# Tiles of 125 partitions moved in two transfers of 112 and 13 partitions, in a two-layer graph network on one core

## The reference, cut to what matters

```
xn = layernorm(x)
x = x + graph0(xn, edges) + linear_attention(xn)
x = x + experts0(layernorm(x))
xn = layernorm(x)
x = x + graph1(xn, edges) + flow_attention(xn)      # graph1: two attention layers over the edges,
x = x + experts1(layernorm(x))                      # the first with 4 heads of 512 features, the second with one of 768
```

## Time and profile before

| | |
|---|---|
| median of 3 runs | 3583.74 us (3577.38 to 3588.89) |
| the profiled execution's own time | 3586.41 us |
| its span | 3584.6 us |
| PE busy | 2857.5 us (80%) |
| DVE busy | 1539.8 us (43%) |
| ACT busy | 809.5 us (23%) |
| mean granted TensorE clock | 0.877 of full speed |
| moved by DMA | 314.12 MB, mean 88 GB/s |

### The profile page before, as it was taken

How to read it: one execution, slowest core, us unless ns; L and a number is a source line. 1 busy time by engine, 2 the same in 40 slices (tenths; PEclk the granted TensorE clock), 3 DMA queues, 4 the chain that set the end, 5 groups by cost and what they waited for, 6 DMA issues and landing times. The chain is left out here.

```text
span 3584.6 us, 32335 instructions
## 1 busy us (share of the span) xinstructions
PE 2857.5 (80%) x12086; PEld 2117.3 (59%) x12086; DVE 1539.8 (43%) x2325; ACT 809.5 (23%) x1117; POOL 259.9 (7%) x251
## 2 busy tenths in 40 slices
PE   4998687989449956999899769995972976928884
PEld 2564355578449934966587535553972536727773
DVE  2214886332425434123227068883126533215554
ACT  1000012020125502211222234442102111014451
POOL 0000000000110020000000033330002200020002
PEclk9999898999569957988799989996985986969996
DMA  4400002120078631100113121103211001066664
GB/s 158 166 14 14 3 17 81 68 96 1 17 255 285 224 96 67 32 18 12 61 62 122 65 85 61 61 30 106 67 54 48 0 1 53 1 182 223 234 214 152
DMA packets 110467, 314.12 MB, mean 88 GB/s; under 512 B 40860, under 2 KB 50741, under 8 KB 101156
## 3 DMA queue, kind: packets, MB, share of 16 engines
q1 hardware_dynamic: 70572, 224.26, 18.1%
q10 hardware_dynamic: 21856, 57.43, 4.3%
q0 software_dynamic: 17920, 30.81, 3.2%
HBM read 215.33 MB, written 97.05 MB: 87 GB/s over the span
## 5 line engine op out<-in xcount | busy, mean ns | idle before, releaser
L2021 PE MATMUL ps<-g_p,g_h 125*128 125x418 f32 x960 | 341.8, 516 | 50.3 <-DMA g_h<-h_projected 50.3
L2021 PEld LDWEIGHTS ps<-g_p,g_h 125*128 125x128 f32 x960 | 182.8, 191 | 207.1 <-issue 156.3
L1043 PE MATMUL ps<-e_wh,e_xh 128*128 128x384 f32 (+1 forms) x600 | 221.0, 368 | 0.5 <-DVE e_wl L1262 0.5
L1043 PE MATMUL ps<-e_wh,e_xl 128*128 128x384 f32 (+1 forms) x600 | 214.7, 358 | 0.0
L1043 PE MATMUL ps<-e_wl,e_xh 128*128 128x384 f32 (+1 forms) x600 | 214.3, 357 | 0.0
L215 PE MATMUL ps<-la_w,normed 128*125 128x384 f32 x480 | 156.6, 490 | 6.7 <-DMA la_w<-in_L_kv 6.7
L1272 DVE TENSOR_TENSOR e_xl<-ps,e_xh 128x768 fp32r<-128x768 f32 x68 | 65.1, 958 | 214.6 <-ACT e_xh L1213 214.6
L1140 PE MATMUL ps<-ident,e_x 128*128 128x128 f32 x408 | 59.1, 284 | 114.1 <-DMA e_x<-expert_rows 114.1
L1043 PE MATMUL ps<-w_hi,h_hi 128*125 128x384 f32 x320 | 114.0, 356 | 42.1 <-DVE w_lo L2609 42.0
L2297 PE MATMUL ps<-g_p,normed 125*128 125x418 f32 x360 | 130.1, 523 | 19.5 <-DVE g_p L2476 19.5
L2112 DVE SCALAR_TENSOR_TENSOR ps<-g_rows,g_logits,normed 125x418 f32<-125x418 f32 x120 | 127.1, 1068 | 33.0 <-DMA g_bias<-in_L_b 15.6
(11 more groups left out here) (413 smaller groups left out, 5825.1 us busy)
## 6 DMA issues: line engine op xcount, KB each, us to landing
e_w<-in_L_experts SPq DMA_DIRECT2D x32, 1152.0 KB, 6.2
e_w<-in_L_experts SPq DMA_DIRECT2D x18, 1536.0 KB, 7.1
e_x<-expert_rows SPq DMA_DIRECT2D x68, 384.0 KB, 5.2
expert_rows<-e_y ACTq DMA_DIRECT2D x68, 384.0 KB, 3.7
expert_rows<-attT ACTq DMA_DIRECT2D x13, 1536.0 KB, 6.6
e_w<-in_L_experts SPq DMA_DIRECT2D x18, 768.0 KB, 5.2
h<-normed SPq DMA_DIRECT2D x48, 209.0 KB, 1.9
h_projected<-gp_h ACTq DMA_DIRECT2D x40, 250.0 KB
```

The source lines that it names most:

```text
L1043: mm = nc.tensor.matmul(out, lhs[a], rhs[b], start=(start and m == 0), stop=(stop and m == 2))
L2021: mm = nc.tensor.matmul(ps[:, f, 0:CW], h_sb[:, i % 2, t, P * f:P * f + P], pr[:, n % 2, t, :], start=(t == 0), stop=(t == TILES - 1))
```

## The change

A helper `two_parts` issues two transfers where there was one: partitions 0 to 111, then partitions 112 to 124, on the same queue, to the same semaphore. Every wait on such a semaphore asks for 32 where it asked for 16. No buffer, order or arithmetic changes. Loads of 125 partitions that are left as they were: the edges, the attention vectors (`a_rows`) and a small bias. There are 41 such transfers on SP (x 2, masks out 10, counts out 1, masks in 10 and 10, counts in 3 and 1, features 4) and 40 on ACT (the feature tiles), so 81 issues more.

```diff
+def two_parts(eng, dst, src, sem):
+
+    for part in (slice(0, 112), slice(112, NT)):
+        eng.dma_start(dst[part], src[part]).then_inc(sem, 16)
...
-                    sp.dma_start(k.x_node[:, 5 * g:5 * g + 5, :],
-                                 x_dram[625 * g:625 * g + 625, :].rearrange("(t p) d -> p t d", p=NT)).then_inc(loaded[g], 16)
+                    two_parts(sp, k.x_node[:, 5 * g:5 * g + 5, :],
+                              x_dram[625 * g:625 * g + 625, :].rearrange("(t p) d -> p t d", p=NT), loaded[g])
...
-                    dve.wait_ge(loaded[t // 5], 16)
+                    dve.wait_ge(loaded[t // 5], 32)
...
-                    sp.dma_start(k.far_dram[t], far[:, t % 2, 0:T]).then_inc(far_out[t % 2], 16)
+                    two_parts(sp, k.far_dram[t], far[:, t % 2, 0:T], far_out[t % 2])
                 for h in range(2):
-                    sp.wait_ge(far_out[h], 16 * (TILES // 2))
+                    sp.wait_ge(far_out[h], 32 * (TILES // 2))
...
-                sp.dma_start(k.counts_dram[:, :, :], whole[:]).then_inc(kept, 16)
+                two_parts(sp, k.counts_dram, whole[:], kept)
...
-                        sp.dma_start(far[:, t % 2, :], k.far_dram[t]).then_inc(far_in[t % 2], 16)
+                        two_parts(sp, far[:, t % 2, :], k.far_dram[t], far_in[t % 2])
...
-                        act.wait_ge(st[n % HR], 16 * (n // HR))
+                        act.wait_ge(st[n % HR], 32 * (n // HR))
...
-                    act.dma_start(h_dram[n // TILES, :, n % TILES, :], h[:, n % HR, :]).then_inc(st[n % HR], 16)
+                    two_parts(act, h_dram[n // TILES, :, n % TILES, :], h[:, n % HR, :], st[n % HR])
...
-                    sp.dma_start(h_sb[:, i % 2], h_dram[i]).then_inc(h_in[i % 2], 16)
+                    two_parts(sp, h_sb[:, i % 2], h_dram[i], h_in[i % 2])
...
-                    sp.dma_start(counts[:, a:b, :], k.counts_dram[:, a:b, :]).then_inc(c_in[q], 16)
+                    two_parts(sp, counts[:, a:b, :], k.counts_dram[:, a:b, :], c_in[q])
...
-                        sp.dma_start(far[:, n % 2, :], k.far_dram[t]).then_inc(far_in[n % 2], 16)
+                        two_parts(sp, far[:, n % 2, :], k.far_dram[t], far_in[n % 2])
...
-                sp.dma_start(counts[:], k.counts_dram[:, :, :]).then_inc(c_in, 16)
+                two_parts(sp, counts[:], k.counts_dram, c_in)
```

More of the change, by code:

```diff
@@ L447, in rows_out @@
                     if t >= 2:
-                        dve.wait_ge(far_out[t % 2], 16 * (t // 2))
+                        dve.wait_ge(far_out[t % 2], 32 * (t // 2))
                     nc.vector.tensor_reduce(k.dinv[:, t:t + 1], st[:, t % 2, 0:T], AX_X, ALU.add).then_inc(summed, 1)
@@ L562, in _ @@
                 sp.wait_ge(cast, TILES)
-                sp.dma_start(k.counts_dram[:, :, :], whole[:]).then_inc(kept, 16)
+                two_parts(sp, k.counts_dram, whole[:], kept)
                 for i in range(1, heads):
                     weights_in(i)
-                sp.wait_ge(kept, 16)
+                sp.wait_ge(kept, 32)
             @block.vector
@@ L1890, in _ @@
                     if n >= HR:
-                        act.wait_ge(st[n % HR], 16 * (n // HR))
+                        act.wait_ge(st[n % HR], 32 * (n // HR))
                     nc.scalar.activation(h[:, n % HR, :], ps[0:NT, n % 4, 0:F], ACT.Copy).then_inc(out, 1)
                     act.wait_ge(out, n + 1)
-                    act.dma_start(h_dram[n // TILES, :, n % TILES, :], h[:, n % HR, :]).then_inc(st[n % HR], 16)
+                    two_parts(act, h_dram[n // TILES, :, n % TILES, :], h[:, n % HR, :], st[n % HR])
                     extra(n)
                 for q in range(HR):
-                    act.wait_ge(st[q], 16 * len(range(q, N, HR)))
+                    act.wait_ge(st[q], 32 * len(range(q, N, HR)))
             @block.vector
@@ L1924, in _ @@
                 for t in range(TILES):
-                    dve.wait_ge(far_in[t % 2], 16 * (t // 2 + 1))
+                    dve.wait_ge(far_in[t % 2], 32 * (t // 2 + 1))
                     for i in range(heads):
@@ L2015, in _ @@
                             if n % CH == 0:
-                                pe.wait_ge(h_in[i % 2], 16 * (i // 2 + 1))
+                                pe.wait_ge(h_in[i % 2], 32 * (i // 2 + 1))
                             pe.wait_ge(s["p_made"], TILES * (n + 1))
@@ L2118, in weights @@
                                 if m == a:
-                                    dve.wait_ge(c_in[q], 16)
+                                    dve.wait_ge(c_in[q], 32)
                             nc.vector.scalar_tensor_tensor(out=pr[:, n % 2, t - 2, :], in0=t1(m), scalar=1.0,
@@ L2433, in maxima @@
                         n = i * TILES + t
-                        dve.wait_ge(far_in[n % 2], 16 * (n // 2 + 1))
+                        dve.wait_ge(far_in[n % 2], 32 * (n // 2 + 1))
                         nc.vector.tensor_tensor_reduce(mscr, rows[0:NT, i % 2, 0, 0:T], far[:, n % 2, :], 1.0, 3 * BIG, ALU.add, ALU.max,
@@ L2520, in _ @@
                 dve.wait_ge(b_in, 16)
-                dve.wait_ge(c_in, 16)
+                dve.wait_ge(c_in, 32)
                 weights(0, 0)
```

## The result

| | before | after |
|---|---|---|
| median of 4 runs of each | 3582.34 us (3577.38 to 3588.89) | 3540.61 us (3534.80 to 3548.74) |
| ratio | | 0.9888, 95% interval 0.9868 to 0.9909 |
| span of the profiled execution | 3584.6 us | 3537.6 us |
| PE busy | 2857.5 us | 2853.5 us |

The kernel is 41.7 us faster by the medians. The forecast was 3530 us with a range of 3516 to 3548: the time lies inside it, but of the 54 us in the sum some 42 came (33 to 47 by the interval of the ratio). The profile after says where the missing 12 are.

What follows compares the result with a forecast made beforehand. Waits for 125-partition transfers, on five of sixteen engines, were taken as what the change could shorten, with PE busy 80%. 20 + 25 + 6.5 + 2.5 = 54 us off 3586.41 gave 3532.4, forecast as 3530 us, range 3516 to 3548.

Steps and rivals of the forecast that it cites:

- No change: Rival: parts of 112 stay on five engines and the issues are hidden; time within 0.3% of the old; chance 0.05.
- a middle spread of eight engines: Rival: the fullest engine has 14 + 2 partitions; about 28 us gained, 3556 us; chance 0.06.
- serial parts: Rival: parts move at the old pace, the second after the first; 20 us added, 3604 us; chance 0.04.
- the share: Sign of being right: DMA share near 0.9 to 1.0 during the load of x, at about 400 GB/s.
- the statistics near 9 us: Sign of being right: DVE's statistics of x begin near 9 us and end near 18 to 21 us.
- DVE's weights as PE's releaser: Sign of being right, first four-head graph layer: weights release PE instead of features; its 50.3 us idle shrinks to about 25.
- the features still release PE: Sign of being wrong, first four-head graph layer: PE still waits for the features, near 2070 us or later.
- 8 x 15,360 bytes at 25.8 GB/s: Step for each half of x: the fullest engine has 8 partitions, so the flow takes 4.8 us instead of 15.2.
- x: Term for the load of x at the start: halves land at 8.9 and 13.7 us, statistics end earlier; 20 us.
- The first four-head layer: Term for counts and features in the first graph layer of four heads: PE starts earlier, at 2066.2; 25 us.
- The masks of the last layer: Term for DVE's two mask buffers: two masks take 5.1 us instead of 6.34; 6.5 us.
- Ends of two stages: Term: last mask wait in the counts stage about 1.3, last ACT store in the projection stage about 1.2; together 2.5 us.

Runs made afterwards that it cites:

- The cut at 115: The same two transfers as in the change, cut at 115 partitions instead of 112; ratio 1.0018 to the kernel before.
- The places run: Six loads of 983,040 bytes without the network, on 16, 32 and 64 partitions, neighbours or spread; 109 against 198, 200 against 384, 204 against 415 GB/s.
- The padded kernel: The kernel before with every transfer that the change cuts as one of 128 partitions, three of them padding; 3531.07 us, ratio 0.9861.

## Why the prediction was right, and what it mis-sized

**The reason held.** Five engines carried a tile of 125 partitions, the parts of 112 use all sixteen (share near 1), and what waited for such a tile gained. The cut at 115 shows that it is the divisor that counts, not that there are two transfers. No change, a middle spread of eight engines and serial parts are out.

Of the signs named beforehand the share, the masks and the projection stage came out, the last with no idle time left in PE's costliest group there:

```profile
L1049 PE MATMUL ps<-gp_w_hi,normed_hi 128*125 128x512 f32 x240 | 96.2, 401 | 0.0
```

The 400 GB/s, the statistics near 9 us and DVE's weights as PE's releaser did not. One sign of being wrong came true: the features still release PE, 26.9 us after the first issue, which on the clock of the kernel before is 2073.

**The step that was mis-sized** is the pace: "8 x 15,360 bytes at 25.8 GB/s". The 25.8 came from loads of 128 partitions. With 112 partitions sixteen engines work, but they move 290 GB/s in the stretch of x shown above instead of 412, and 247 over the load of the four-head layer. The places run shows that the pace depends on which partitions are written. That with 112 several engines meet at one place of the on-chip memory and wait for each other fits this, but it is inferred: that run had no load of 112. The bounds were taken from one kind of row, and both ends (25.8 and 20.7 GB/s for each engine) came from transfers of 128 partitions, so they did not bound this case. Term by term:

- *x*: forecast 20 us, bounds 18.4 to 20.8; measured 13.6, and 12.9 for the whole when done alone.
- *The first four-head layer*: forecast 25, bounds 22 to 26; measured 18.4, and 17 when done alone. 125 x 45,560 bytes at 247 GB/s are 23.1 us; with the 2.2 of fixed time and four issues more the features come 26.6 us after the first issue (measured 26.9). DVE's own path was forecast well, but the features still come after it.
- *The masks of the last layer*: forecast 6.5, bounds 3.8 to 9. Two masks take 4.92 where 5.1 was said, but the step that the counts of this layer cost nothing was wrong: the wait for the attention vectors is 2.6 us longer, some 2 of it by the counts in parts. From the issue of the bias to the load behind the layer the stage is 5.7 us shorter (2664.91 to 2951.48 before, 2628.56 to 2909.45 after).
- *Ends of two stages*: forecast 2.5, bounds 0 to 3; measured 4.3, above the upper bound. The projection stage is 3.2 us shorter (201.86 to 198.65 from its first issue to that of the next stage). 1.4 of it is PE's idle time that went, which the prediction had put at nothing. The counts stage is 2.4 us shorter (189.18 to 186.77), but the stage behind it, which stores the counts and was put at nothing, is 1.3 longer (141.77 to 143.04): 1.1 in all. The forty issues more on ACT, 0.34 us each by the median, cost PE nothing there.

13.6 + 18.4 + 5.7 + 3.2 + 1.1 are 42.0 us, and the medians differ by 41.7. The two profiled spans, from which the terms are read, differ by 47.0. The rest lies in stages that the change does not touch, and they go both ways. The flow attention took 6.7 us less in this profile of the changed kernel (364.71 against 371.40) but 371.39 in the other one, so this is chance. From the load of the router's weights to the first of the experts it took 4 us more (104.06 against 100.03), and 103.28 in the other profile. In the three other kernels that change every transfer this stretch is 101.8 to 103.4 us, in the three that change one group of loads 98.7 to 99.7. So there is a side effect of some 2 to 5 us that the sum lacks, and no run shows its cause.

The padded kernel gives the two large terms their forecast size (20.3 us for x, since the statistics end at 18.9, and 45.3 - 20.0 = 25.3 in the four-head layer), so with the pace of 128 partitions both sums hold. Its whole gain is 49.7 us by the ratio (41 to 59 by the interval).

**What was luck.** That the time lies inside the range is in part luck. The gain of 41.7 us is below the 44 of the lower bounds, and both large terms are below their own. The range was counted from one profiled execution of 3586.41 us, while the median before is 3582.34; from that median a gain of 44 us would have given 3538, and the time of 3540.61 would have needed the margin of 6 us that was added at that end.

**What stays open.** Why 120 partitions on fifteen engines are slower (195 GB/s) than 112 on sixteen (289) is not settled by a run: the order in which each engine takes its partitions may decide it, and the trace does not show it. Why 112 stay at 289 is open in the same way. The pace of the part of 13 inside the stream is not separated from that of 112 either. If 112 partitions flow at 289 GB/s there as they do by themselves, the half of x takes 5.95 us for them, and 1.78 are left for 0.2 MB, an estimate of 112 GB/s.

## What to carry to other kernels

Look for tiles whose partition count has only small divisors: a DMA share of 0.32 while something waits was five engines of sixteen here. Give such a tile the full 128 partitions, with padding if need be, rather than a split: the split earns about 42 us here, and padding, with one more small load brought to 128, 15 to 20 more for a few unread bytes, where the input can be had in padded tiles. Cut only the loads that something waits for: the counts of the last layer in parts made another load later. And take a pace only from a transfer on the same partitions; a share near 1 is no proof of full pace, so read the GB/s beside it.

## What the runs showed of the hardware that was not expected

With sixteen engines at work and the same source, the pace of a load depended on the partitions written, by a factor of about two within each pair of the same count and of four over all: 109 GB/s on partitions 0 to 15, 198 on every eighth, 200 on 0 to 31, 384 on every fourth, 204 on 0 to 63 and 415 on every second. 112 partitions from 0 moved 289 and 120 moved 195. A younger transfer also went with a later landing of an older one: DVE's wait for the attention vectors went from 9.6 us to 12.2 with the masks and counts behind it in parts, and was 10.0 with the counts whole.
